# A recommender tower on one core: context's term in one stacked fp32r pass, fewer early lookups, and two more tiles in the plain form

## The chip, the cores and the metric

The kernel runs on one core of one Trainium2 chip. The metric is device time in microseconds, the median of repeated runs. Engines are called as in the profile: PE is TensorE (PEld its weight loads), DVE is VectorE, ACT is ScalarE, POOL is GpSimd, SP is SyncE.

## What is computed

The inputs are 1024 samples. For each, 39 table lookups of 16 numbers give `e` (1024 x 39 x 16). Two layers of products between fields follow, then a sum over the 16 positions, and a small dense network on top:

```python
def _cin_layer(x0, xk, W, b):
    out = jnp.einsum('bhd,bmd,shm->bsd', xk, x0, W) + b[None, :, None]
    return jax.nn.relu(out)
x1 = _cin_layer(x0, x0, W1, b1)          # W1: 128 x 39 x 39
x2 = _cin_layer(x0, x1, W2, b2)          # W2: 128 x 128 x 39
z = jnp.concatenate([x1.sum(axis=-1), x2.sum(axis=-1)], axis=-1)
h = jnp.concatenate([z, dense_ctx], axis=1)          # 256 + 16 features
h = jnp.maximum(h @ W_top1 + b_top1, 0.0)            # 512
h = jnp.maximum(h @ W_top2 + b_top2, 0.0)            # 256
y = h @ W_top3
```

## The kernel before, in words

The samples are cut into 32 tiles of 32; a tile has 512 columns (32 samples x 16 positions) and is worked off in two pairs, so there are 64 pairs. Precision is kept with fp32r matmuls on split operands: a value is split into a high part (an fp32r copy, made by ACT) and a low part (the value less its high part), and a product is the sum of high x high, high x low and low x high. A matmul on plain fp32 operands leaves two records in the profile.

**The way of a tile.** POOL looks up its rows (`look_up`, L418, ten indirect DMAs for each tile, semaphore `s_look`). SP copies them in place with 16 DMAs (L411, `s_put`); for the first two tiles DVE and ACT do it. POOL multiplies out 15 of the products (`multiplied_out`, L361). ACT makes the high part (`high_part`, L604) and two copies of the products' high part (`products_high`, L610); POOL makes the low parts (`low_parts`, L369). All lands in `e_hl`, a ring of 8 buffers. PE transposes it (`turn`, L817). Then come seven steps of layer 1 (`layer1_at`, L859): an expanding matmul (L837), a square on ACT (`square`, L573), and a matmul that adds it up. From tile SOON = 4 on, a square is split: ACT makes the high part and the full square (L584, L585), DVE the low part (L717), and PE runs three fp32r matmuls (L850, L851, L853). Tiles before SOON use one fp32 matmul (L855). ACT and DVE then make the layer's result with its parts (L593, L596, L721).

**The second layer.** A pair has 39 fields, in banks of four: 7 banks "D" that DVE multiplies and adds up (L769, 54 operations a pair, and two at the end, L792 and L796), and 3 banks "A" that ACT scales (L552) and POOL adds up (`middle_fields`, `four_to_two`, `last_two`, `whole_sum`, all L431) to `fsum`. Each bank is 6 fp32r matmuls on PE (L881, L882, L885) into a ring of three: before a bank, PE waits until the bank three places earlier is drained (L876). The order of a pair's ten slots is written out: `DDADDADDAD`. DVE starts a pair from `fsum`; for pairs before LATE = 4 it starts from zero and adds `fsum` at the end (L782).

**What sets the order.** Every engine's program is laid out by pair p and slot s (0 to 9). `layer1_steps` says which layer 1 step stands behind which slot; `high_slots(p)` behind which slots ACT makes the high parts; `split_pair(t)` in which pair tile t is split; `turn_step` where it is transposed; `lookups(p)` how many lookups POOL makes in round p (one at a time between its adds, L503 to L539). POOL's round p holds the adds of pair p + 1. An engine does its instructions in order, so a wait stops all that stands behind it.

**The top layers** run for samples 0 to 511 during pairs 34 to 37, for 512 to 959 during pairs 60 to 63, and for the last 64 at the end. In layer 1 each of four steps has three fp32 matmuls (L914): the two sums, and the context with 16 rows.

Of the kernel before, what the change touches and what calls it, by code (L numbers as in the profile page):

```python
# [11 lines left out]
F32R = mybir.dt.float32r  # L12
# [4 lines left out]
S = 128  # L17
CTX = 16
F1, F2 = 512, 256

# [11 lines left out]
LOOKED = 8  # L32


SOON = 4

# [24 lines left out]

LATE = 4
SLOTS = len(ORDER)
# [120 lines left out]
def lookups(p):  # L184

    return 7 if p < 6 else 6


def high_slots(p):

    return (6, 7) if p == 0 else (0, 1) if SPLIT_IN[p] < SOON else (3, 6)

# [37 lines left out]
def cin_tower(nc, table, ids_first, ids, first_row, w1a, w1b, fold, w2, b2, sel, ident, rows_sum, wt1, wt1c, bt1, wt2, bt2, wt3, ctx_t, out):  # L230
    with ExitStack() as stack:
# [13 lines left out]
        prod = sb("prod", [P, LOOKED, ZP * DT])  # L245
        e_hl = sb("e_hl", [P, LOOKED, P, DT])
        x0t = sb("x0t", [P, 2, N], F32R)
# [31 lines left out]
        wt1_sb = sb("wt1_sb", [P, 2, F1])  # L279
        wt1c_sb = sb("wt1c_sb", [CTX, F1])  # L280
        wt2_sb = sb("wt2_sb", [P, F1 // P, F2])
        wt3_sb = sb("wt3_sb", [P, F2 // P])
        ctx_sb = sb("ctx_sb", [CTX, B])

# [10 lines left out]
        s_const = sem("s_const")  # L295
        s_mlpw = sem("s_mlpw")
        s_rows = sem("s_rows")
        s_look = [sem(f"s_look{t}") for t in range(TILES)]
# [70 lines left out]
        def low_parts(engine, t):  # L369

            done, hl = s_el_first if t < FIRST_TILES else s_el, e_hl[:, t % LOOKED, :, :].rearrange("p m d -> p (m d)")
            engine.wait_ge(s_eh, 3 * t + 1)
            engine.tensor_tensor(hl[:, M * DT:2 * M * DT], e[:, t, :, :].rearrange("p m d -> p (m d)"), hl[:, 0:M * DT],
                                 ALU.subtract).then_inc(done, 1)
            engine.wait_ge(s_eh, 3 * t + 2)
            engine.tensor_tensor(hl[:, ZL * DT:(ZL + ZP) * DT], prod[:, t % LOOKED, :], hl[:, ZH * DT:(ZH + ZP) * DT],
                                 ALU.subtract).then_inc(done, 1)
# [13 lines left out]
        with nc.Block() as block:  # L391
# [25 lines left out]
            def _(pool):  # L417
# [83 lines left out]
                for p in range(PAIRS):  # L501
                    mine, then = SPLIT_IN.get(p), p + 1
                    mine_soon = mine is not None and mine < SOON  # L503
                    ahead = iter(range(n, min(n + lookups(p), TILES * LOOKUPS)))
                    n += lookups(p)

                    def look_ahead(count):
                        for k in itertools.islice(ahead, count):
                            look_up(k)

                    if mine_soon:
                        multiplied_out(nc.gpsimd, mine)
                    look_ahead(1)
                    if mine is not None and not mine_soon:
                        multiplied_out(nc.gpsimd, mine)
                    if then < PAIRS:
                        middle_fields(then)
                    look_ahead(1)
                    if mine_soon:
                        low_parts(nc.gpsimd, mine)  # L520
                    if then < PAIRS:
                        four_to_two(then, 2, 1, 0)
                    look_ahead(1)
                    if then < PAIRS:
                        four_to_two(then, 3, 2, 8)
                    look_ahead(1)
                    if then < PAIRS:
                        last_two(then)
                    look_ahead(1)
                    if then < PAIRS:  # L530
                        whole_sum(then)
                    if p % 2 == 0 and p // 2 + 1 < TILES:
                        position_sum(p // 2 + 1)
                    look_ahead(1)
                    if mine is not None and not mine_soon:
                        low_parts(nc.gpsimd, mine)
                    if p + 2 < PAIRS:
                        first_fields(p + 2)
                    look_ahead(lookups(p))  # L539
# [3 lines left out]
            def _(act):  # L543
# [60 lines left out]
                def high_part(t):  # L604
                    wait_put(act, t)
                    if t >= LOOKED:
                        act.wait_ge(s_full, STAGED["turn", t - LOOKED] + 1)
                    nc.scalar.activation(e_hl[:, t % LOOKED, 0:M, :].bitcast(F32R), e[:, t, :, :], ACT.Copy).then_inc(s_eh, 1)

                def products_high(t):  # L610
# [7 lines left out]
                    for row in (ZH, ZW):  # L618
                        nc.scalar.activation(e_hl[:, t % LOOKED, row:row + ZP, :].bitcast(F32R), src, ACT.Copy).then_inc(s_eh, 1)

# [42 lines left out]
                for p in range(PAIRS):  # L663
                    mine = SPLIT_IN.get(p)
                    for s in range(SLOTS):
# [11 lines left out]
                        for kind, q, j in BANK_SLOTS[1 + SLOTS * p + s]:  # L677
                            if kind == "A":
                                scaled_fields(q, j)
                            elif kind == "L":  # L680
                                last_scaled_fields(j)
                        if mine is not None and s == high_slots(p)[0]:
                            high_part(mine)
# [16 lines left out]
            def _(dve):  # L700
# [11 lines left out]
                def square_low(t, v):  # L712
                    k = C1 * t + v
                    dve.wait_ge(s_sq, splits(t, v))
                    if k >= 2:
                        dve.wait_ge(s_mm1, k - 1)
                    nc.vector.tensor_tensor(zl[:, k % 2, :], ps[:, BK_T, :], zh[:, k % 2, :], ALU.subtract).then_inc(s_zl, 1)  # L717

                def first_layer_low(t):
# [32 lines left out]
                for p in range(PAIRS):  # L752
                    n = p * STT_PER_PAIR
                    last = d_banks(p) - 1
                    for j in range(last + 1):
# [19 lines left out]
                        for at in split_after(p, j):  # L775
                            square_low(*at)
                    for sub in range(2):
                        x2 = ps[:, 2 * (nth % RING) + sub, k * S:(k + 1) * S]
# [21 lines left out]
            def _(pe):  # L800
# [16 lines left out]
                def turn(t):  # L817
# [6 lines left out]
                    for d in range(DT):  # L824
                        mm = nc.tensor.transpose(ps[:, BK_T, d * P:(d + 1) * P],  # L825
                                                 e_hl[:, t % LOOKED, :, d], ident_sb[:])
                    mm.then_inc(s_full, 1)
# [67 lines left out]
                def mlp(g, layer, c):  # L895
                    lo, hi = GROUPS[g]
                    f, y = slice(c * P, (c + 1) * P), ps[:, BK_T, 0:hi - lo]
                    if layer == 1:
                        if c == 0:
                            pe.wait_ge(s_mlpw, 16 * len(mlp_weights))  # L900
                            pe.wait_ge(s_p2t, hi // BT)
                            pe.wait_ge(s_p1, P1_OPS * hi // BT)
                        terms = [(wt1_sb[:, 0, f], p1[:, lo:hi]), (wt1_sb[:, 1, f], p2t[:, lo:hi]),
                                 (wt1c_sb[:, f], ctx_sb[:, lo:hi])]
                    elif layer == 2:
# [43 lines left out]
                pe.wait_ge(s_p1, P1_OPS * TILES)  # L949
                pe.wait_ge(s_mlpw, 16 * len(mlp_weights))  # L950
                for c in range(F1 // P):
                    f = slice(c * P, (c + 1) * P)
# [4 lines left out]
                    nc.tensor.matmul(ps[:, TAIL_1[c], 0:n], wt1_sb[:, 0, f], p1[:, lo:hi], start=True, stop=False)  # L957
                    nc.tensor.matmul(ps[:, TAIL_1[c], 0:n], wt1c_sb[:, f], ctx_sb[:, lo:hi], start=False, stop=False)
                sums(TILES - 1)
# [88 lines left out]
```

## Time and profile before

| | us |
|---|---|
| median of 3 runs | 1210.94 (1210.28 to 1210.98) |
| the profiled execution | 1209.32 |
| its span in the profile | 1207.3 |
| PE busy | 1162.2 |
| DVE busy | 1075.3 |
| POOL busy | 900.6 |
| ACT busy | 692.3 |

The profile shows one execution. Busy times of PE are times in which a matmul is in flight; matmuls are pipelined, so the distance from one start to the next says more than a record's length. A wait is put down to the instruction that came last before it ended.

### The profile page before, as it was taken

How to read it: one execution, taken by the hardware profiler on the slowest of the kernel's cores; microseconds unless marked ns; L12 is line 12 of the kernel's file. 1: busy time of each engine (PE TensorE's matmuls, PEld its weight loads, DVE VectorE, ACT ScalarE, POOL GpSimd, SP SyncE). 2: the span in 40 equal slices, each digit the busy share in tenths (PEclk: the TensorE clock that was granted, in tenths of full speed). 3: DMA queues.
4: the chain of work that ended last, by engine and by line, in shares of the span. 5: the costliest groups of instructions: out<-in, count | busy, mean ns of one | idle time of the engine just before them, and what ended most of it. 6: DMA issues, size and time to landing. Idle time of an engine off the chain costs nothing.

```text
span 1207.3 us, 18938 instructions
## 1 busy us (share of the span) xinstructions
PE 1162.2 (96%) x4952; PEld 898.9 (74%) x4952; DVE 1075.3 (89%) x3811; ACT 692.3 (57%) x2177; POOL 900.6 (75%) x930
## 2 busy tenths in 40 slices
PE   3897999999999999999999999999999999999998
PEld 2575777777777777777777677777778777777766
DVE  4476899999999999999999779999999999999966
ACT  3554565656666556666565555566666566656432
POOL 7898998888888888888887676888876454645432
PEclk9998999999999999999999999999999999999998
DMA  5111111111111111111111100111110000000000
GB/s 180 8 7 7 7 8 6 7 6 7 6 7 8 7 6 7 6 6 7 7 7 6 6 5 5 7 7 7 7 6 2 1 1 1 1 1 1 1 1 1
DMA packets 170249, 11.58 MB, mean 10 GB/s; under 512 B 163630, under 2 KB 169262, under 8 KB 170013
## 3 DMA queue, kind: packets, MB, share of 16 engines
q1 hardware_dynamic: 159901, 7.73, 7.5%
q0 software_dynamic: 10240, 2.64, 2.8%
q8 instruction: 39, 0.64, 0.2%
q14 instruction: 69, 0.57, 0.2%
HBM read 7.92 MB, written 0.00 MB: 7 GB/s over the span
## 4 chain that ended last, share of the span: by engine, by line
PE 59%; DVE 16%; ACT 12%; issue 6%; POOL 6%; DMA 0%; POOLq 0%; DVEq 0%; ACTq 0%; SPq 0%
PE ps L881 16%; PE ps L882 15%; DVE acc L769 15%; PE ps L885 14%; ACT fy L552 9%; POOL looked L422 4%; PE ps L914 3%; PE ps L837 2%; ACT ps L585 2%; ACT zh L584 1%; PE ps L850 1%; PE ps L851 1%; PE ps L853 1%; PE ps L825 1%; POOL fsum L431 1%
## 5 line engine op out<-in xcount | busy, mean ns | idle before, releaser
L769 DVE SCALAR_TENSOR_TENSOR acc<-ps,e,acc 128x128 f32<-128x128 f32 x3186 | 846.9, 342 | 76.6 <-PE ps L885 70.6
L431 POOL TENSOR_TENSOR fy<-fy 128x512 f32<-128x512 f32 (+1 forms) x256 | 403.0, 1574 | 204.7 <-ACT fy L552 196.3
L881 PE MATMUL ps<-w2h,x1h 128*128 128x512 f32 (+1 forms) x1280 | 523.3, 409 | 21.2 <-ACT fy L552 9.9
L882 PE MATMUL ps<-w2l,x1h 128*128 128x512 f32 (+1 forms) x1280 | 496.3, 388 | 0.0
L885 PE MATMUL ps<-w2h,x1l 128*128 128x512 f32 (+1 forms) x1280 | 495.5, 387 | 0.4 <-DVE x1l L721 0.4
L552 ACT ACTIVATE fy<-ps,e 128x128 f32<-128x128 f32 x1536 | 415.8, 387 | 83.0 <-PE ps L885 82.9
L422 POOL DMA_INDIRECT looked<-in_table,rows x320 | 311.6, 974 | 58.3 <-POOL fy L431 23.4
L881 PEld LDWEIGHTS ps<-w2h,x1h 128*128 128x128 f32 x1280 | 241.5, 189 | 125.9 <-DVE acc L769 33.9
L885 PEld LDWEIGHTS ps<-w2h,x1l 128*128 128x128 f32 x1280 | 241.1, 188 | 49.6 <-DVE x1l L721 0.9
L882 PEld LDWEIGHTS ps<-w2l,x1h 128*128 128x128 f32 x1280 | 241.7, 189 | 43.7 <-issue 4.7
L584 ACT ACTIVATE zh<-ps 128x512 fp32r<-128x512 f32 x168 | 103.7, 617 | 247.2 <-PE ps L837 243.2
L717 DVE TENSOR_TENSOR zl<-ps,zh 128x512 fp32r<-128x512 f32 x168 | 114.9, 684 | 9.7 <-ACT ps L585 8.4
L585 ACT ACTIVATE ps<-ps 128x512 f32<-128x512 f32 x168 | 103.7, 617 | 0.0
L837 PE MATMUL ps<-x0t,sel_r 78*128 78x512 f32 x186 | 74.2, 399 | 0.9 <-ACT z L587 0.9
L850 PE MATMUL ps<-zh,w1h 128*128 128x512 f32 x168 | 66.9, 398 | 0.0
L851 PE MATMUL ps<-zh,w1l 128*128 128x512 f32 x168 | 66.4, 395 | 0.0
L853 PE MATMUL ps<-zl,w1h 128*128 128x512 f32 x168 | 66.1, 394 | 0.0
L431 POOL TENSOR_TENSOR fy<-fy,b_sb 128x256 f32<-128x256 f32 x64 | 47.4, 741 | 11.5 <-ACT fy L552 10.8
L431 POOL TENSOR_TENSOR fsum<-fy 128x256 f32<-128x256 f32 x64 | 47.7, 745 | 3.8 <-DVE acc L769 1.7
L593 ACT ACTIVATE x1h<-ps 128x512 fp32r<-128x512 f32 x32 | 19.1, 598 | 43.4 <-PE ps L853 41.7
L769 DVE SCALAR_TENSOR_TENSOR acc<-ps,e,fsum 128x128 f32<-128x128 f32 x120 | 36.2, 343 | 8.5 <-POOL fsum L431 8.5
L837 PEld LDWEIGHTS ps<-x0t,sel_r 78*128 78x128 f32 x186 | 34.9, 188 | 9.1 <-ACT z L587 2.7
(87 smaller groups left out, 624.4 us busy)
## 6 DMA issues: line engine op xcount, KB each, us to landing
e<-looked SPq DMA_DIRECT2D x360, 5.0 KB, 1.9
looked<-in_table,rows POOLq DMA_INDIRECT x320, 2.4
e<-looked SPq DMA_DIRECT2D x120, 4.5 KB, 1.9
w_st<-in_w SPq DMA_DIRECT2D x1, 1728.0 KB, 10.1
wt_sb<-in_wt SPq DMA_DIRECT2D x2, 512.0 KB, 4.1
w_st<-in_w SPq DMA_DIRECT2D x1, 768.0 KB, 5.9
w_sb<-in_w1a SPq DMA_DIRECT2D x1, 448.0 KB, 3.2
w1b_sb<-in_w1b SPq DMA_DIRECT2D x1, 448.0 KB, 3.9
```

The lines of the kernel that those rows point to most:

```text
L422: nc.gpsimd.indirect_dma_start(looked[:, t % LOOKED, j, :], None, table, bass.IndirectOffsetOnAxis(rows[:, t, j:j + 1], 0)).then_inc(s_loo ...
L431: nc.gpsimd.tensor_tensor(out, a, b, ALU.add).then_inc(s_fsum, 1)
L552: nc.scalar.activation(fy[:, p % 2, sub, m - MD, :], ps[:, 2 * (nth % RING) + sub, k * S:(k + 1) * S], ACT.Copy, scale=emb(p, sub, m)).the ...
L584: nc.scalar.activation(zh[:, k % 2, :], src, ACT.Square).then_inc(s_z1, 1)
L585: nc.scalar.activation(src, src, ACT.Square).then_inc(s_sq, 1)
L717: nc.vector.tensor_tensor(zl[:, k % 2, :], ps[:, BK_T, :], zh[:, k % 2, :], ALU.subtract).then_inc(s_zl, 1)
L769: nc.vector.scalar_tensor_tensor(acc[:, sub, :] if m < fields("D", last)[-1] else y, y, emb(p, sub, m), acc[:, sub, :] if m else fsum[:, p ...
L837: nc.tensor.matmul(ps[:, BK_T, :], sel_r[:, v, :], x0t[0:2 * M, t % 2, :], start=True, stop=True).then_inc(s_full, 1)
L850: nc.tensor.matmul(ps[:, BK_ACC1, :], w1h[:, v, :], zh[:, k % 2, :], start=False, stop=False)
L881: nc.tensor.matmul(y, x1h[:, t % 2, at], w2h[:, cols], start=True, stop=False)
L882: nc.tensor.matmul(y, x1h[:, t % 2, at], w2l[:, cols], start=False, stop=False)
L885: mm = nc.tensor.matmul(y, x1l[:, t % 2, at], w2h[:, cols], start=False, stop=True)
```

## The change

Context's term: the host lays the 16 context rows and the 16 weight rows out three times, at rows 0, 32 and 64 of arrays of 80 rows, with zeros between. ACT copies both to fp32r (`context_high`, in pair 14 behind slot 9), DVE puts the low parts of the context into rows 32 to 47 (at the end of pair 16) and those of the weights into rows 64 to 79 (at the end of pair 18). One fp32r matmul of 80 rows then gives the three products.

Early pairs: SOON goes from 4 to 6, so tiles 4 and 5 take the unsplit form; their steps stand every two slots from slot 11 of their tile's stretch on (before: every three from slot 6), their high parts are made in pairs 4 and 6 (before: 3 and 5) behind slots 1 and 4, and they are transposed at slot 0 of the next pair. Tile 3's high parts move from slots 0 and 1 of pair 2 to slots 4 and 5. POOL's low parts of tile 3 move ahead of `middle_fields`. Lookups go from 7 in each of rounds 0 to 5 to 6, 5, 5, 5, 6, 6. LATE goes from 4 to 7. `e_hl` has 4 buffers instead of 8.

```diff
-SOON = 4
+HELD = 4
+SOON = 6
-LATE = 4
+LATE = 7
 def lookups(p):
-    return 7 if p < 6 else 6
+    return 6 if p == 0 or p >= 4 else 5
 def high_slots(p):
-    return (6, 7) if p == 0 else (0, 1) if SPLIT_IN[p] < SOON else (3, 6)
+    return (6, 7) if p == 0 else (4, 5) if p == 2 else (1, 4) if SPLIT_IN[p] < SOON else (3, 6)
+CONTEXT_AT, CONTEXT_LOW = (14, 9), (16, 18)
...
-        e_hl = sb("e_hl", [P, LOOKED, P, DT])
+        e_hl = sb("e_hl", [P, HELD, P, DT])
-        wt1c_sb = sb("wt1c_sb", [CTX, F1])
+        wt1c_sb = sb("wt1c_sb", [CTX_K, F1])
+        wt1c_r = sb("wt1c_r", [CTX_K, F1], F32R)
-        ctx_sb = sb("ctx_sb", [CTX, B])
+        ctx_sb = sb("ctx_sb", [CTX_K, B])
+        ctx_r = sb("ctx_r", [CTX_K, B], F32R)
...
                         multiplied_out(nc.gpsimd, mine)
+                    if p == 2:
+                        low_parts(nc.gpsimd, mine)
                     if then < PAIRS:
                         middle_fields(then)
                     look_ahead(1)
-                    if mine_soon:
+                    if mine_soon and p != 2:
                         low_parts(nc.gpsimd, mine)
...
                 def high_part(t):
                     wait_put(act, t)
-                    if t >= LOOKED:
-                        act.wait_ge(s_full, STAGED["turn", t - LOOKED] + 1)
+                    if t >= HELD:
+                        act.wait_ge(s_full, STAGED["turn", t - HELD] + 1)
...
+                def context_high():
+                    act.wait_ge(s_mlpw, 16 * len(mlp_weights))
+                    nc.scalar.activation(ctx_r[:], ctx_sb[:], ACT.Copy).then_inc(s_ctxh, 1)
+                    nc.scalar.activation(wt1c_r[:], wt1c_sb[:], ACT.Copy).then_inc(s_ctxh, 1)
...
+                        if (p, s) == CONTEXT_AT:
+                            context_high()
...
+                def context_low():
+                    rows = slice(CTX_ROWS[1], CTX_ROWS[1] + CTX)
+                    dve.wait_ge(s_ctxh, 1)
+                    nc.vector.tensor_tensor(ctx_r[rows, :], ctx_sb[rows, :], ctx_r[rows, :], ALU.subtract).then_inc(s_ctxl, 1)
+
+                def context_weights_low():
+                    rows = slice(CTX_ROWS[2], CTX_ROWS[2] + CTX)
+                    dve.wait_ge(s_ctxh, 2)
+                    nc.vector.tensor_tensor(wt1c_r[rows, :], wt1c_sb[rows, :], wt1c_r[rows, :], ALU.subtract).then_inc(s_ctxl, 1)
...
+                    if p == CONTEXT_LOW[0]:
+                        context_low()
+                    elif p == CONTEXT_LOW[1]:
+                        context_weights_low()
                     for sub in range(2):
                         x2 = ps[:, 2 * (nth % RING) + sub, k * S:(k + 1) * S]
...
                             pe.wait_ge(s_mlpw, 16 * len(mlp_weights))
+                            pe.wait_ge(s_ctxl, 2)
...
-                                 (wt1c_sb[:, f], ctx_sb[:, lo:hi])]
+                                 (wt1c_r[:, f], ctx_r[:, lo:hi])]
...
-                    nc.tensor.matmul(ps[:, TAIL_1[c], 0:n], wt1c_sb[:, f], ctx_sb[:, lo:hi], start=False, stop=False)
+                    nc.tensor.matmul(ps[:, TAIL_1[c], 0:n], wt1c_r[:, f], ctx_r[:, lo:hi], start=False, stop=False)
...
+    for row in CTX_ROWS:
+        wt1c[row:row + CTX], ctx_t[row:row + CTX] = x["W_top1"][2 * S:], x["dense_ctx"].T
```

## Rows read from the trace of the kernel before

**Rows 1.** The page: busy time by engine, share of the span, instructions.
```profile
PE 1162.2 (96%) x4952; PEld 898.9 (74%) x4952; DVE 1075.3 (89%) x3811; ACT 692.3 (57%) x2177; POOL 900.6 (75%) x930
```
**Rows 2.** Stretches: from:to, length, busy by engine (instructions), PE clock, DMA share, GB/s.
```profile
300.00:334.90 34.90, 34.55 (x153) 27.30 (x152) 33.53 (x121) 21.24 (x67) 29.98 (x32) 1.00 0.14 7
```
**Rows 3.** Waits: waiter, what it waited for, us in total, times, longest.
```profile
DVE acc L769 <- PE ps L885: 70.6, 57, 9.0
```
**Rows 4.** Timeline of PE, 92 to 102 us: start, length, instruction [idle before].
```profile
92.74 0.39 PE L885 MATMUL ps<-w2h,x1l 128*128 128x512 f32 x1
100.57 0.79 PE L881 MATMUL ps<-w2h,x1h 128*128 128x512 f32 x1 [7.44 <-ACT fy L552]
```
**Rows 5.** Stretches, columns as in rows 2.
```profile
100.60:104.60 4.00, 4.00 (x11) 3.26 (x12) 0.00 (x0) 0.80 (x4) 3.83 (x4) 0.51 0.18 6
```
**Rows 6.** Timeline of ACT, 84 to 101 us.
```profile
90.84 0.34 ACT L608 ACTIVATE e_hl<-e 128x156 fp32r<-128x156 f32 x1 [4.29 <-DMA e<-looked]
...
98.06 0.40 ACT L619 ACTIVATE e_hl<-prod 128x60 fp32r<-128x60 f32 x2 [5.92 <-POOL prod L367]
98.36 2.15 ACT L552 ACTIVATE fy<-ps,e 128x128 f32<-128x128 f32 x8
```
**Rows 7.** Timeline of SP's DMA issues, 70 to 95 us.
```profile
77.52 11.38 SPq L411 DMA_DIRECT2D e<-looked  x16
```
**Rows 8.** Timeline of POOL, 79 to 99 us.
```profile
96.73 0.96 POOL L422 DMA_INDIRECT looked<-in_table,rows  x1 [0.16 <-POOL fy L431]
97.71 0.32 POOL L367 TENSOR_TENSOR prod<-e 128x60 f32<-128x60 f32 x1
```
**Rows 9.** Timeline of DVE, 84 to 113 us.
```profile
105.67 5.26 DVE L769 SCALAR_TENSOR_TENSOR acc<-ps,e,acc 128x128 f32<-128x128 f32 x20 [9.04 <-PE ps L885]
...
112.43 0.60 DVE L766 TENSOR_SCALAR acc<-ps,e 128x128 f32<-128x128 f32 x2
```
**Rows 10.** Timeline of PE, 74 to 78 us.
```profile
75.94 0.40 PE L837 MATMUL ps<-x0t,sel_r 78*128 78x512 f32 x1
76.18 1.02 PE L855 MATMUL ps<-z,w_sb 128*128 128x512 f32 x2
...
77.27 0.40 PE L882 MATMUL ps<-w2l,x1h 128*128 128x512 f32 x1
```
**Rows 11.** Stretches, columns as in rows 2.
```profile
112.40:219.00 106.60, 105.59 (x458) 82.84 (x456) 99.12 (x357) 63.28 (x200) 94.92 (x100) 1.00 0.14 7
```
**Rows 12.** Timeline of POOL, 154 to 172 us.
```profile
154.26 0.33 POOL L367 TENSOR_TENSOR prod<-e 128x60 f32<-128x60 f32 x1
...
171.18 2.41 POOL L431 TENSOR_TENSOR fy<-fy 128x1024 f32<-128x1024 f32 x1
```
**Rows 13.** Timeline of POOL, 146.5 to 151 us.
```profile
147.99 0.74 POOL L480 TENSOR_TENSOR xs<-x 128x256 f32<-128x256 f32 x1
...
150.14 0.96 POOL L422 DMA_INDIRECT looked<-in_table,rows  x1
```
**Rows 14.** Timeline of PE, 653 to 657 us.
```profile
653.54 1.02 PE L914 MATMUL ps<-p,wt_sb 128*128 128x512 f32 x2
...
655.35 1.12 PE L914 MATMUL ps<-ctx_sb,wt1c_sb 16*128 16x512 f32 x2
656.40 0.50 PE L881 MATMUL ps<-w2h,x1h 128*128 128x512 f32 x1
656.74 0.40 PE L882 MATMUL ps<-w2l,x1h 128*128 128x512 f32 x1
```
**Rows 15.** Timeline of DVE, 1128 to 1190 us.
```profile
1176.05 2.16 DVE L769 SCALAR_TENSOR_TENSOR acc<-ps,e,acc 128x128 f32<-128x128 f32 x8 [2.24 <-PE ps L885]
```
**Rows 16.** Groups of instructions by shape: count, busy us, mean ns, idle before.
```profile
L730 DVE TENSOR_TENSOR w_sb<-w_sb,w1b_sb 128x896 f32<-128x896 f32 x1 | 1.1, 1092 | 2.7 <-DMA fold_sb<-in_fold 2.7
```
**Rows 17.** Timelines of DVE and POOL, 19.5 to 31 us.
```profile
23.72 3.76 DVE L709 SCALAR_TENSOR_TENSOR w2l<-w_st,w2h 128x3456 fp32r<-128x3456 f32 x1
...
24.11 4.19 POOL L422 DMA_INDIRECT looked<-in_table,rows  x1 [0.30 <-issue]
```

More of the change, by code:

```diff
@@ L18 @@
 CTX = 16
+CTX_ROWS = (0, 32, 64)
+CTX_K = CTX_ROWS[-1] + CTX
 F1, F2 = 512, 256
@@ L296, in cin_tower @@
         s_mlpw = sem("s_mlpw")
+        s_ctxh = sem("s_ctxh")
+        s_ctxl = sem("s_ctxl")
         s_rows = sem("s_rows")
@@ L369, in low_parts @@
         def low_parts(engine, t):
-            done, hl = s_el_first if t < FIRST_TILES else s_el, e_hl[:, t % LOOKED, :, :].rearrange("p m d -> p (m d)")
+            done, hl = s_el_first if t < FIRST_TILES else s_el, e_hl[:, t % HELD, :, :].rearrange("p m d -> p (m d)")
             engine.wait_ge(s_eh, 3 * t + 1)
@@ L605, in high_part @@
                     wait_put(act, t)
-                    if t >= LOOKED:
-                        act.wait_ge(s_full, STAGED["turn", t - LOOKED] + 1)
-                    nc.scalar.activation(e_hl[:, t % LOOKED, 0:M, :].bitcast(F32R), e[:, t, :, :], ACT.Copy).then_inc(s_eh, 1)
+                    if t >= HELD:
+                        act.wait_ge(s_full, STAGED["turn", t - HELD] + 1)
+                    nc.scalar.activation(e_hl[:, t % HELD, 0:M, :].bitcast(F32R), e[:, t, :, :], ACT.Copy).then_inc(s_eh, 1)
                 def products_high(t):
@@ L618, in products_high @@
                     for row in (ZH, ZW):
-                        nc.scalar.activation(e_hl[:, t % LOOKED, row:row + ZP, :].bitcast(F32R), src, ACT.Copy).then_inc(s_eh, 1)
+                        nc.scalar.activation(e_hl[:, t % HELD, row:row + ZP, :].bitcast(F32R), src, ACT.Copy).then_inc(s_eh, 1)
+                def context_high():
+                    act.wait_ge(s_mlpw, 16 * len(mlp_weights))
+                    nc.scalar.activation(ctx_r[:], ctx_sb[:], ACT.Copy).then_inc(s_ctxh, 1)
+                    nc.scalar.activation(wt1c_r[:], wt1c_sb[:], ACT.Copy).then_inc(s_ctxh, 1)
                 def sums_turned(t):
@@ L825, in turn @@
                         mm = nc.tensor.transpose(ps[:, BK_T, d * P:(d + 1) * P],
-                                                 e_hl[:, t % LOOKED, :, d], ident_sb[:])
+                                                 e_hl[:, t % HELD, :, d], ident_sb[:])
                     mm.then_inc(s_full, 1)
@@ L950, in _ @@
                 pe.wait_ge(s_mlpw, 16 * len(mlp_weights))
+                pe.wait_ge(s_ctxl, 2)
                 for c in range(F1 // P):
@@ L1025 @@
     first_row = np.repeat(first_row.reshape(LOOKUPS, Q).T, BT, axis=0)
+    wt1c, ctx_t = np.zeros((CTX_K, F1), np.float32), np.zeros((CTX_K, B), np.float32)
+    for row in CTX_ROWS:
+        wt1c[row:row + CTX], ctx_t[row:row + CTX] = x["W_top1"][2 * S:], x["dense_ctx"].T
     arrays = {
@@ L1031 @@
         "sel": selection(), "ident": np.eye(P, dtype=np.float32), "rows_sum": np.tile(np.eye(BT, dtype=np.float32), (Q, 1)),
-        "wt1": x["W_top1"][:2 * S].reshape(2, S, F1).transpose(1, 0, 2), "wt1c": x["W_top1"][2 * S:],
+        "wt1": x["W_top1"][:2 * S].reshape(2, S, F1).transpose(1, 0, 2), "wt1c": wt1c,
         "bt1": x["b_top1"].reshape(F1 // P, P).T,
@@ L1036 @@
         "wt3": x["W_top3"].reshape(F2 // P, P).T,
-        "ctx_t": x["dense_ctx"].T,
+        "ctx_t": ctx_t,
     }
```

## The prediction

> **What bounds the kernel now.** I read the page first: the matmul engine is busy for 96% of the span, VectorE for 89%, GpSimd for 75% [rows 1]. A busy matmul engine proves little by itself, so next came the table of stretches. One tile (two pairs) takes 34.9 us in the middle of the run, with 34.55 us busy on PE and 33.53 us on DVE [rows 2]: both are nearly full, PE sets the pace, and DVE follows so closely that a microsecond more on it in one place will mostly show. The table of waits then says where time is lost in one piece: DVE waited 9.0 us once for PE [rows 3]. The timeline of PE shows the hole behind it, 7.44 us of waiting for ACT's scaling, from 92.97 to 100.57 us [rows 4], in pair 2 before its slot 5 (L881 needs the bank that ACT drains at L552). Behind it the clock is at 0.51, the lower level of 1.2 GHz, for 4 us; its 11 matmul records run at half speed, which costs some 2 us [rows 5].
>
> Why was ACT late? Its timeline in pair 2 has two waits ahead of the scaling: 4.29 us for tile 3's placed rows (L608), then 5.92 us for tile 3's products from POOL (L619) [rows 6]. SyncE issues the 16 copies of tile 3 in 11.4 us and is done at 88.9 [rows 7]; POOL comes to the products only at 97.71, because adds and lookups stand before them without a gap [rows 8]. So the early hole is ACT's order (the high part at slots 0 and 1) and POOL's load.
>
> **The change, part by part.** All against the profiled execution (1209.3 us), which is 1.6 us under the median of 1210.9.
>
> (a) High part of tile 3 at slots 4 and 5, and its low parts moved up on POOL. ACT first does first_layer(2) and the scaling for slot 2, so the wait for the copies stops nothing that PE needs before slot 7. POOL loses one lookup in pair 0 and two in pair 1; one is 0.98 us from start to start, 0.16 us more where a start gap goes with it [rows 8], so 3.4 us for three, and the products come at 94.3 instead of 97.71. ACT is at slot 5 until about 96.8 (the bank is ready at 94.6, eight scalings are 2.2 us [rows 6]), so the product copy no longer waits; POOL's low_parts(3) waits for it until about 97.2, some 1.4 us, with middle_fields(3) behind it in POOL's queue, which even so starts at 97.5 and not at 100.6. What is late next is DVE: it stood 9.04 us before 105.67, and needs 6.76 us from there to the start of pair 3 at 112.43 [rows 9]. Without the hole PE would deliver pair 2's last bank at about 100.1, so DVE runs on from 96.6 and starts pair 3 at 103.4. Gain 9.0 us; the clock's 2 us lie inside it, since DVE becomes the bound for a moment.
>
> (b) SOON from 4 to 6: tiles 4 and 5 take the plain fp32 form. On PE a step's one fp32 matmul (two records) takes 0.86 us: from 76.18 to 77.27 less the 0.23 of the matmul that follows [rows 10]. It takes the place of three fp32r ones at 0.23, 0.69 in all; 12 steps x 0.17 = 2.0 us more. In return DVE loses 12 subtractions, which stood at 0.6 us each, and ACT 12 squares. The stretch of pairs 3 to 8 holds 105.59 us of PE work in 106.6 [rows 11], but with restarts after DVE's waits of about 0.1 each inside the busy time; I take 1.3 us of waits to go. Net cost 0.7 us; bounds 2.0 (no wait goes) and -0.3.
>
> (c) LATE from 4 to 7 adds two small DVE operations in pairs 4 to 6 (some 0.25 us of spacing each, 1.5 us) and takes away their wait for fsum at the start. DVE has 7 us more room there by (b): nothing, up to 0.5 if DVE is full after all.
>
> (d) Lookups. POOL took 16.9 us for the round from one product (154.26) to the next middle_fields (171.18), with seven lookups and one low_parts [rows 12]: 6.9 for the lookups and 1.1 for products and low parts leave 8.9 for the adds; even rounds have 2.15 for position_sum as well [rows 13]. Laid end to end behind low_parts(3) at 97.5 (four lookups left, adds, position_sum: 112.4; then five and adds: 126.2; six and all: 144.2; six and adds: 159.0) POOL comes to the products of tile 4 at 126.2 and of tile 5 at 159.0. PE starts pair 3 at 100.9, and needs 13.5 us for a pair's banks (60 matmuls at 0.23, six of them shorter), with a turn and five steps of 1.09 some 18.6, with the last two steps 15.9: pair 4 at 119.5, pair 6 at 153.9. ACT wants the products four slots later, at 127.2 and 161.3. fsum(7) comes 13.5 us into round 6, at 172.5, where DVE wants it at about 172. All fit, none by much. Tile 3's last lookup keeps its place, so its copies land as before. Tile 6's last lookup comes in pair 6 and its copies end at about 176.5, where ACT wants them at 175.5: inside the ring's three slots. Lookups end one pair later: 0.2 us.
>
> (e) HELD 4 halves the memset at the start, which lies ahead of a DMA wait: nothing. The bigger context arrays add 0.38 MB to SyncE's burst at 19 us; the next lookups that anybody waits for end at 32 us: nothing, at most 0.5.
>
> (f) Context term in one pass. Before, context's matmul takes 655.35 to 656.40, and the L881 behind it 0.34 us instead of 0.23; ahead of it stands 0.09 (the first two take 1.72 of the 1.81 us from 653.54) [rows 14]. So one step spends 1.05 + 0.11 + 0.09 = 1.25 us on it, where an fp32r pass costs 0.23. Saving 1.02 for each of four steps, and by columns (448 of 512) 0.89 for each of the next four: 7.6 us. These bubbles of 0.2 to 0.3 stand only around this 16-row load; the 128-row fp32 steps at L855 have none [rows 10]. If they stayed, the saving would be the columns alone, 0.86 - 0.23 = 0.63 and 0.55: 4.7 us, the lower bound. I take the upper one, 7.6, since the 78-row fp32r matmul at L837, nearest to the new pass in form and rows, also runs free of them: the next one starts 0.24 us behind it [rows 10]. PE is the bound in both stretches: even in the last pairs DVE waits 2.24 us for it at 1176 [rows 15], so what PE saves reaches the end. The tail's context matmuls lie before a wait for DVE: nothing.
>
> (g) Splitting context. ACT makes two copies (1.0 and 0.6 us) in pair 14, between squares three slots apart: hidden. DVE has 1024 and 512 columns at the ends of pairs 16 and 18. The nearest row is an add of 896 columns, 1.09 us [rows 16], which gives 1.2 and 0.65: 1.85 less the overlap, 1.7 us. It stands before the drain of the pair's last bank, and DVE had 1.4 us of room in a whole tile; bounds 0.3 and 1.9, I take 1.7.
>
> Here a rule speaks against the change. A POOL lookup that met DVE's long low-part operation (23.72, 3.76 us, two inputs from SBUF) took 4.19 us [rows 17] instead of 0.96 [rows 8]. A delay like that at pairs 16 and 18 would be at most the two operations' own length, 1.9 us on POOL, and counts only if fsum becomes late by it. The Trainium skill, SBUF — State Buffer, section on who interferes with whom, says that a VectorE instruction with two SBUF inputs and a GpSimd instruction that reads SBUF shut each other out for the whole instruction. By that rule, the sum would be up to 1.9 us worse; the trace agrees that such waits happen.
>
> Sum: -9.0 + 0.7 + 0.2 - 7.6 + 1.7 = -14.0, so 1195.3 for a profiled execution and 1196.9 for the median; I say 1197.0.
>
> **Rivals.**
> 1. The hole moves instead of going. Ahead of slot 44 and slot 64 ACT needs POOL's products, with margins of only 1 to 3 us in (d), and turn(3) needs low_parts(3). Against it: the ring covers three slots, some 4 us. Half of (a) lost: -9.5, 1201.5.
> 2. The lockout of [rows 17] comes fully on the path: 1.9 us more, 1198.9. Against it: at odd pairs DVE rarely waits for fsum.
> 3. Slower than before: POOL falls behind for good in pairs 2 to 6, since it now stands waiting for ACT in pair 2. The point is a product copy (slot 44) that waits more than 4.2 us, three slots of 1.4; I reckon below 0.5. Then (a)'s 9.0 stays lost and one more hole of 9.0 opens: +9.0 + 0.7 + 0.2 - 7.6 + 1.7 = +4.0, 1214.9.
> 4. The change doesn't do what it says: the stacked pass costs as much as the fp32 one. Then only (a) to (e) and (g) count: -6.4, 1204.5. Against it: the fp32r matmul at L837 has 78 rows and takes 0.24 us [rows 10].
>
> **How the numbers follow.** A measurement of this kernel tells 0.2% (2.4 us) from no change. Forecast 0.64, rival 1 0.15, rival 2 0.10, rival 3 0.04, rival 4 0.04; 0.03 for a total near zero. The range starts from the sum of the better bounds (-9.0 - 0.3 + 0.2 - 7.6 + 0.3 = -16.4, 1194.5, with 2 us for DVE waits that I had as full cost) at 1192.5, and reaches to 1204.0, which takes in rivals 1 and 2 and the worse bounds together (-9.0 + 2.0 + 0.5 + 0.2 + 0.5 - 4.7 + 1.9 = -8.6, 1202.3). Faster 0.93, same 0.03, slower 0.04.
>
> **What would show it.** In the new profile: PE without a hole above 1 us in 92 to 102 us and the clock at 1.00 there; pair 3 starts on DVE near 103.4; the product copy of tile 3 without a wait, POOL waiting 1.4 us before low_parts(3); L855 with 72 records instead of 48; the tile period at 34.9 us as before; four steps of L914 near 675 and four near 1145 each 0.9 to 1.0 us shorter, context as single records; a DVE operation of 1.2 us near 348 us with a PE wait of about 1 us behind it. The forecast is wrong if a PE wait above 2 us stands anywhere between 100 and 200 us, if the tile period of the middle differs from 34.9 us, or if bubbles stay around the context matmul.

## The result, and the profile after

The changed kernel takes 1196.01 us in the median (four runs, 1195.4 to 1197.02) where the kernel before takes 1210.96 (1210.28 to 1211.69): ratio 0.9877, 95% interval 0.986 to 0.9894. The profiled execution took 1195.4, its span 1193.6, so 13.7 us less span. The forecast was 1197.0, its range 1192.5 to 1204.0.

The page and the waits that stood first [rows 1, 3], of the changed kernel (waits: waiter, what it waited for, us in total, times, longest):

```profile
PE 1152.4 (97%) x4928; PEld 894.1 (75%) x4928; DVE 1071.0 (90%) x3807; ACT 689.9 (58%) x2167; POOL 904.2 (76%) x930
```
```profile
DVE acc L801 <- PE ps L921: 63.5, 64, 5.2
```

PE has 9.8 us less busy time for 13.7 us less span, and the longest wait of DVE for PE fell from 9.0 to 5.2. Where the hole stood [rows 4, 5, 2], the table of stretches (from:to, length, busy by engine, PE clock, DMA share, GB/s) and PE's timeline now show:

```profile
92.00:102.00 10.00, 9.33 (x43) 7.36 (x42) 9.98 (x38) 5.02 (x21) 9.32 (x12) 1.00 0.03 3
300.00:334.90 34.90, 34.57 (x152) 27.26 (x151) 33.48 (x120) 22.73 (x69) 29.95 (x32) 1.00 0.11 6
```
```profile
100.28 0.50 PE L917 MATMUL ps<-w2h,x1h 128*128 128x512 f32 x1 [0.67 <-DVE acc L801]
```

The clock is 1.00 where it was 0.51, PE's longest wait in these 10 us is 0.67 and is for DVE, PE waits nowhere over 1 us between 85 and 200 us, and the middle of the run is what it was. ACT and POOL in pair 2 [rows 6, 8]:

```profile
89.89 2.18 ACT L567 ACTIVATE fy<-ps,e 128x128 f32<-128x128 f32 x8 [0.30 <-issue]
91.91 0.38 ACT L623 ACTIVATE e_hl<-e 128x156 fp32r<-128x156 f32 x1
...
96.23 0.45 ACT L634 ACTIVATE e_hl<-prod 128x60 fp32r<-128x60 f32 x2
```
```profile
94.58 0.33 POOL L380 TENSOR_TENSOR prod<-e 128x60 f32<-128x60 f32 x1
...
96.07 0.54 POOL L386 TENSOR_TENSOR e_hl<-e,e_hl 128x156 f32<-128x156 f32 x1
...
96.89 2.40 POOL L444 TENSOR_TENSOR fy<-fy 128x1024 f32<-128x1024 f32 x1
```

ACT scales first and copies afterwards; neither the copy of the rows nor that of the products waits (4.29 and 5.92 us before).

To see where the 13.7 us come from I took the start of every pair on DVE in both traces. The gain (before less after), summed up to that pair:

| pair | 0 | 2 | 3 | 5 | 9 | 16 | 17 | 19 | 34 | 38 | 60 | 62 | span |
|---|---|---|---|---|---|---|---|---|---|---|---|---|---|
| us | -0.36 | 0.54 | 9.67 | 10.95 | 8.62 | 8.50 | 7.11 | 6.21 | 5.93 | 9.89 | 9.45 | 13.08 | 13.7 |

Each step of the prediction has its place in it: the hole (pair 2 to 3), the two plain tiles (to 9), the subtractions (16 to 17 and 18 to 19), the two groups of the top layer (34 to 38, 60 to 62). The 0.54 us before pair 2 and the 0.63 behind pair 62 belong to no step; the steps and what lies between them come to 12.5 us.

### The profile page after: what moved, and what is told of

Same layout as the page of the kernel before. It is cut to its first block, busy times and chain, and to the rows that moved or that the text cites. A ratio compares the mean times of both kernels' runs of the same rounds, so it can differ in the third digit from the quotient of the medians.

```text
span 1193.6 us, 18875 instructions
## 1 busy us (share of the span) xinstructions
PE 1152.4 (97%) x4928; PEld 894.1 (75%) x4928; DVE 1071.0 (90%) x3807; ACT 689.9 (58%) x2167; POOL 904.2 (76%) x930
## 4 chain that ended last, share of the span: by engine, by line
PE 64%; DVE 13%; ACT 12%; issue 6%; POOL 4%; DMA 0%; POOLq 0%; ACTq 0%; SPq 0%; DVEq 0%
PE ps L917 18%; PE ps L918 16%; PE ps L921 16%; DVE acc L801 12%; ACT fy L567 9%; POOL looked L435 3%; PE ps L951 3%; PE ps L873 3%; PE ps L891 2%; ACT ps L600 1%; PE ps L886 1%; PE ps L887 1%; PE ps L889 1%; ACT zh L599 1%; PE ps L861 1%
## 5 line engine op out<-in xcount | busy, mean ns | idle before, releaser
L918 PE MATMUL ps<-w2l,x1h 128*128 128x512 f32 (+1 forms) x1280 | 495.1, 387 | 0.0
L918 PEld LDWEIGHTS ps<-w2l,x1h 128*128 128x128 f32 x1280 | 240.7, 188 | 46.6 <-issue 7.6
L599 ACT ACTIVATE zh<-ps 128x512 fp32r<-128x512 f32 x156 | 96.4, 618 | 228.9 <-PE ps L873 228.9
L739 DVE TENSOR_TENSOR zl<-ps,zh 128x512 fp32r<-128x512 f32 x156 | 106.6, 683 | 8.4 <-ACT ps L600 6.5
L600 ACT ACTIVATE ps<-ps 128x512 f32<-128x512 f32 x156 | 96.2, 617 | 0.0
L886 PE MATMUL ps<-zh,w1h 128*128 128x512 f32 x156 | 61.9, 397 | 0.0
L887 PE MATMUL ps<-zh,w1l 128*128 128x512 f32 x156 | 61.7, 395 | 0.0
L889 PE MATMUL ps<-zl,w1h 128*128 128x512 f32 x156 | 61.4, 393 | 0.0
L602 ACT ACTIVATE z<-ps 128x512 f32<-128x512 f32 x36 | 21.9, 610 | 40.5 <-PE ps L873 34.7
```

Of the source, the lines that this page charges most:

```text
L599: nc.scalar.activation(zh[:, k % 2, :], src, ACT.Square).then_inc(s_z1, 1)
L600: nc.scalar.activation(src, src, ACT.Square).then_inc(s_sq, 1)
L886: nc.tensor.matmul(ps[:, BK_ACC1, :], w1h[:, v, :], zh[:, k % 2, :], start=False, stop=False)
L918: nc.tensor.matmul(y, x1h[:, t % 2, at], w2l[:, cols], start=False, stop=False)
```

## The experiments

Three sets ran, each with the kernel before on the same chip. In the first two it took 1210.3 and 1210.7 us. In the third it took 1214.7, and the profiled kernels of that set all lose 6.1 to 7.4 us on the changed kernel's trace between pairs 0 and 1, ahead of all that is studied; why stays open. Its four kernels are therefore compared with each other, and one of them stands for the changed kernel. The changed kernel itself ran in none of the three sets: where x5, x6 and x8 are set against its median, two sets are compared in which the kernel before differs by 0.2 us. "The gain at pair n" is as in the table above.

**The two halves alone.** x1 is the changed kernel with the early pairs as before (SOON 4, LATE 4, lookups, `high_slots` and the place of the low parts undone); x2 is the kernel before with just these five.

> The kernel before with the context part of the change alone (stacked pass, its copies and subtractions, four buffers of e_hl; SOON, LATE, lookups, slots and low parts as before). My theory: the two parts are independent, since the early hole closes long before the context is touched. The pass gives 7.6 us, the tail 0.6, the two subtractions on DVE cost 2.3 (1.39 and 0.88 as seen in the changed kernel): 5.9 us less than before, near 1203.4 in a profiled execution, with the 7.4 us hole still at 93 us. Rival: part of the 13.7 us came from an interplay, and this alone gives under 4 us.

> The kernel before with the early part alone (SOON 6, LATE 7, fewer lookups, tile 3's slots and low parts; context as before). My theory: pair 3 starts on DVE 9.0 to 9.7 us earlier, 1.0 is lost again by pair 9, 0.4 by the later end of the lookups: 8.2 us less than before, near 1201.1. Rival: the shorter fill of e_hl and the context's place matter in the early stretch, then it gives under 7 us.

x1: 1204.42, ratio 0.9952 (0.9935 to 0.9969), 5.9 us less than before. From pair 16 to 19 it loses 2.26, from 34 to 38 it gains 3.88, from 60 to 62 3.63. x2: 1202.04, ratio 0.9929 (0.9913 to 0.9946), 8.2 us less; 8.54 at pair 3, 7.53 at pair 9. The two add up to 14.1 of the 14.95 in medians. In spans they give only 5.0 and 6.6 of the 13.7, but 1.6 of the missing 2.2 lie before pair 2 and behind pair 62, which no step touches. Step by step they agree with the whole: 9.14 against 9.13 from pair 2 to 3, 2.26 lost against 2.29 from 16 to 19, 3.88 less 0.12 against 3.96 from 34 to 38, 3.63 less 0.19 against 3.63 from 60 to 62. No interplay larger than these differences is to be seen.

**One piece of the early half at a time.** x3, the kernel before with

```diff
-    return (6, 7) if p == 0 else (0, 1) if SPLIT_IN[p] < SOON else (3, 6)
+    return (6, 7) if p == 0 else (4, 5) if p == 2 else (0, 1) if SPLIT_IN[p] < SOON else (3, 6)
```

> The kernel before with one edit: tile 3's high parts behind slots 4 and 5 of pair 2 instead of 0 and 1. Theory A (ACT's order makes the hole): the 7.4 us hole is gone; what is late next is POOL's low_parts(3), which still stands behind an add and a lookup, so the transposition at slot 30 waits some 2 us; pair 3 starts 7 us earlier, total 6 to 7 us less. Theory B (POOL's load makes the hole): POOL still reaches the products at 97.7, and the hole shrinks by under 3 us.

1210.3, ratio 1.0 (0.9989 to 1.001); the profiled execution was its quickest, 1208.1. Theory A has the hole right and the total wrong; theory B has the hole wrong. The hole of pair 2 goes as in the whole change, 9.22 us at pair 3, and 7.8 of them are lost again at once: 1.42 at pair 4. DVE's and PE's timelines of x3:

```profile
129.65 0.61 DVE L769 SCALAR_TENSOR_TENSOR acc<-ps,e,fsum 128x128 f32<-128x128 f32 x2 [6.77 <-POOL fsum L431]
```
```profile
131.86 0.79 PE L881 MATMUL ps<-w2h,x1h 128*128 128x512 f32 x1 [5.42 <-DVE acc L769]
```

POOL was always late: the kernel before gets this sum at 131.06, x3 at 129.65, hardly sooner. Before, the hole gave it the time, and DVE waited 0.47 us for the sum. With the hole gone and LATE at 4, DVE stands at the start of pair 4 for POOL's sum, and PE behind DVE.

x4, the kernel before with only fewer lookups:

```diff
-    return 7 if p < 6 else 6
+    return 6 if p == 0 or p >= 4 else 5
```

> The kernel before with one edit: the lookups of the changed kernel (6, 5, 5, 5, 6, 6 instead of 7 in rounds 0 to 5). Theory A: ACT still waits for tile 3's copies until 90.8 and then for the products, which now come at 94.6 instead of 97.7; the hole shrinks by 3.1 to about 4.3 us, total 3 to 4 us less. Theory B: the hole nearly goes, total 7 us or more less.

1217.01, ratio 1.0055 (1.0035 to 1.0075), 6.7 us slower; both theories had it faster. The hole shrinks from 7.44 to 4.75 us, near theory A's 4.3, and then ACT stands for the rows of tiles 4 and 5, whose high parts are still due in pairs 3 and 5; the gain falls from 3.58 at pair 3 to -7.18 at pair 6. ACT's timeline of x4:

```profile
120.69 0.33 ACT L608 ACTIVATE e_hl<-e 128x156 fp32r<-128x156 f32 x1 [6.25 <-DMA e<-looked]
...
161.47 0.34 ACT L608 ACTIVATE e_hl<-e 128x156 fp32r<-128x156 f32 x1 [4.91 <-DMA e<-looked]
```

**One piece taken back.** x5 is the changed kernel with `SOON = 4`, x6 with `LATE = 4`, x8 with the lookups of before (7 in rounds 0 to 5).

> The changed kernel with SOON back at 4: tiles 4 and 5 in the split form. PE saves 12 x 0.17 = 2.0 us of matmuls. Theory A (my term b: SOON 6 costs PE 2.0 and gives back waits for DVE): with DVE and ACT full again in pairs 3 to 8, waits for DVE come back, and the total is within 1 us of the changed kernel. Rival: the plain form is a pure cost once the hole is gone, and the total falls by 2 us. Second rival: without DVE's room the two more late adds make DVE the bound, and the total rises by over 1.5 us.

> The changed kernel with LATE back at 4: pairs 4 to 6 start from fsum. Theory A: POOL gives fsum(4) at 123.9, fsum(5) near 139 and fsum(6) near 155.6, where DVE starts at 120.8, 137.9 and 156.0: DVE waits 3 us at pair 4, 1 to 2 at pair 5, and since DVE has room in odd pairs about 2 us of it stay; total 1 to 3 us more. Rival: LATE is worth nothing (under 0.5 us), as I had it.

> The changed kernel with the lookups of before (7 in each of rounds 0 to 5). Tests the margin of rival 1 and 3: POOL is up to 3.4 us later in pair 2 and falls back 2 us more in each of rounds 2 and 3. Theory A (three slots of room, 4.2 us, then PE stops): the products of tile 3 come at 98 where ACT wants them at 96.2, low parts at 99.6: below 1 us at pair 3; by pair 4 POOL is 7 to 8 us late, products of tile 4 come near 132 where ACT wants them at 125: PE stops for 3 us or more there, total 2 to 5 us more. Rival: POOL's idle time takes it up, and the total stays within 1 us.

x5: 1207.34, ratio 0.9972 (0.9958 to 0.9985), 11.3 us more than the changed kernel's median. The second rival had the direction, no theory the cause or the size. ACT's and PE's timelines of x5:

```profile
120.18 0.33 ACT L623 ACTIVATE e_hl<-e 128x156 fp32r<-128x156 f32 x1 [10.56 <-DMA e<-looked]
```
```profile
121.05 0.80 PE L873 MATMUL ps<-x0t,sel_r 78*128 78x512 f32 x1 [5.13 <-ACT z L602]
...
162.16 0.50 PE L917 MATMUL ps<-w2h,x1h 128*128 128x512 f32 x1 [2.39 <-ACT fy L567]
```

Tile 4's rows are in place at 120.2, since its last lookup now comes a round later. With SOON 4 ACT asks for them at 109.6, in pair 3; with SOON 6 at 122.78, in pair 4, and waits for nothing. Tile 5's rows are late too, by 4.68 us at 158.71, with PE's second wait behind them. That, more than its arithmetic, is what SOON 6 is for (x9 below takes the two apart).

x6: 1198.37, ratio 0.9897 (0.9868 to 0.9926), 2.4 us more than the changed kernel by medians (two executions, and the intervals of the ratios overlap), 2.0 by spans and 1.9 by the starts of pairs 3 to 9: at the start of pair 4 DVE waits for the sum that LATE 7 lets it add at the end.

```profile
124.11 0.61 DVE L801 SCALAR_TENSOR_TENSOR acc<-ps,e,fsum 128x128 f32<-128x128 f32 x2 [3.01 <-POOL fsum L444]
```

x8: 1204.14, ratio 0.9942 (0.9919 to 0.9964), 8.1 more by medians and 7.0 by spans, where theory A had the cause but only 2 to 5 us. It loses nothing before pair 4, 5.5 in pair 4 (the gain is 10.08 at pair 4 and 5.32 at pair 5, where the changed kernel has 10.22 and 10.95), and 7.2 by pair 7. So the hole of pair 2 needs no fewer lookups to close (9.14 us from pair 2 to 3); they matter from pair 4 on. ACT's and PE's timelines of x8:

```profile
133.33 0.40 ACT L634 ACTIVATE e_hl<-prod 128x60 fp32r<-128x60 f32 x2 [5.36 <-POOL prod L380]
```
```profile
136.03 0.76 PE L917 MATMUL ps<-w2h,x1h 128*128 128x512 f32 x1 [3.42 <-ACT fy L567]
```

This is the mechanism of rival 3: a wait of ACT of 5.36 us opened a hole of 3.42 on PE, where ACT's waits of 2.56 us for tile 4's rows and 2.36 for its products in x3 opened none. Two other runs lie between: ACT's 4.68 us for tile 5's rows in x5 opened 2.39 on PE, and its 4.91 in x4 opened 2.61.

```profile
164.92 0.50 PE L881 MATMUL ps<-w2h,x1h 128*128 128x512 f32 x1 [2.61 <-ACT fy L552]
```

Each hole is 1.9 to 2.3 us shorter than the wait behind it. The point therefore lies between 2.56 and 4.68 us, and by these differences nearer the lower end than rival 3's 4.2, three slots of 1.4.

**The context pass.** x7 is the kernel before, fp32 matmuls and all, with the context arrays padded with zeros from 16 to 80 rows (no split, no fp32r):

```diff
-        wt1c_sb = sb("wt1c_sb", [CTX, F1])
-        ctx_sb = sb("ctx_sb", [CTX, B])
+        wt1c_sb = sb("wt1c_sb", [80, F1])
+        ctx_sb = sb("ctx_sb", [80, B])
```

> The kernel before with context still one plain fp32 matmul, but over 80 rows, of which 64 are zeros. It separates the two reasons for the 1.01 us that a step saved. Theory A: the bubbles around the context matmul (0.09 ahead, 0.21 behind) come with the 16-row weight load, and go with 80 rows: a step takes 2.81 us instead of 3.20 from the first matmul to the second one behind it, total 2 to 2.5 us less than before. Theory B: they come with the order (fp32 to fp32r, or the wait behind the step): a step stays at 3.2 us, total within 0.5 us of before.

1207.47, ratio 0.9973 (0.9959 to 0.9986): 3.3 us less by medians, 2.8 by spans, though it only multiplies more zeros. PE's timeline, first of x7, then of the changed kernel (before: [rows 14]):

```profile
653.87 1.02 PE L914 MATMUL ps<-p,wt_sb 128*128 128x512 f32 x2
...
655.59 1.02 PE L914 MATMUL ps<-ctx_sb,wt1c_sb 80*128 80x512 f32 x2
656.05 0.79 PE L881 MATMUL ps<-w2h,x1h 128*128 128x512 f32 x1
656.68 0.39 PE L882 MATMUL ps<-w2l,x1h 128*128 128x512 f32 x1
```
```profile
647.59 1.02 PE L951 MATMUL ps<-p,wt_sb 128*128 128x512 f32 x2
...
648.91 0.80 PE L951 MATMUL ps<-ctx_r,wt1c_r 80*128 80x512 f32 x1
...
649.78 0.40 PE L918 MATMUL ps<-w2l,x1h 128*128 128x512 f32 x1
```

From the step's first matmul to the L882 (L918) behind it: 3.20 us before, 2.81 padded, 2.19 in one fp32r pass. The other three steps of the first group give 0.30 to 0.38 and 0.64 to 0.65 for the two differences. So 0.3 to 0.4 us a step are bubbles that belong to the 16-row matmul and go with 80 rows in fp32 as well; 0.62 to 0.65 is the pass itself. No number of rows between 16 and 80 was tried.

**The move of the low parts, and the price of the plain form** (third set). x12 is the changed kernel with tile 3's low parts back behind `middle_fields`; x9 has tiles 4 and 5 split again, at the slots of SOON 6:

```diff
 def is_split(t, v):
-    return t >= SOON and v in SPLIT
+    return t >= 4 and v in SPLIT
```

> The changed kernel with POOL's low parts of tile 3 back behind middle_fields and a lookup. Theory A: POOL then ends them at 100.5, and the transposition at slot 30 starts at about 101.7: nothing waits, total within 0.5 us of the changed kernel; the move had worth only as insurance. Rival: they end later than slot 30 and PE waits, total 1 us or more up.

> The changed kernel, with the squares of tiles 4 and 5 split again but everything at the changed kernel's slots (steps every two slots, high parts in pairs 4 and 6). It separates SOON's arithmetic from its schedule. Theory A (what SOON 6 bought is the later due slot of the copies, seen when SOON 4 cost 12 us; the plain form costs PE 2.0): PE has 2.0 us less, DVE 7.2 us and ACT 6 us more in pairs 5 to 8, DVE becomes the bound there, total within 1.5 us of the changed kernel either way. Rival: the plain form itself is what the early pairs need, and the total rises by over 4 us.

x12: 1201.65, ratio 0.9892 (0.9872 to 0.9911). Against the changed kernel's trace its shift is flat through the place of the move, 6.75 us at pair 1 and 6.70 at pair 9: the move is worth nothing here. POOL made the low parts at 103.78, and the transposition at 108.51 did not wait for them. x12 therefore stands for the changed kernel in this set.

x9: 1203.96, ratio 0.9911 (0.9891 to 0.993), 2.3 us more than x12 by medians (two executions each, and the intervals overlap) and 1.6 by spans. Its shift grows by 1.6 over pairs 5 to 9. The stretch of pairs 5 to 8, first of x9 and then of the changed kernel:

```profile
144.50:218.60 74.10, 71.01 (x313) 56.59 (x311) 69.49 (x246) 45.50 (x139) 61.74 (x66) 1.00 0.15 7
```
```profile
137.90:210.40 72.50, 71.28 (x301) 54.84 (x299) 62.63 (x234) 39.53 (x127) 61.74 (x66) 1.00 0.15 7
```

PE is busy 0.3 us less in x9, not 2.0 as worked out for the fp32r form, and stands idle 3.1 us of the stretch instead of 1.2. DVE is busy 6.9 us more; 1.6 us is what it comes to.

**A better place for the subtractions.** In the changed kernel DVE waits 1.67 us for PE in each of pairs 3, 5 and 7 (its operation at 113.33, 148.43 and 184.55), where tiles 3, 4 and 5, in the plain form, ask no low part of it. x10 puts the two subtractions there:

```diff
-CONTEXT_AT, CONTEXT_LOW = (14, 9), (16, 18)
+CONTEXT_AT, CONTEXT_LOW = (4, 6), (5, 7)
...
+                        if (p, j) == (CONTEXT_LOW[0], 3):
+                            context_low()
+                        elif (p, j) == (CONTEXT_LOW[1], 3):
+                            context_weights_low()
```

x11 has `LATE = 8` in addition, so that DVE adds pair 7's sum at the end.

> The changed kernel with context's copies in pair 4 behind slot 6, and its two subtractions on DVE in pairs 5 and 7 behind the fourth bank, where DVE waits 1.67 us for PE each time. Theory: the 1.39 and 0.88 us that they cost at pairs 16 and 18 go, since they fall into waits: 2.0 to 2.3 us less than the changed kernel, near 1193.3 in a profiled execution. Rival: the pair of subtractions costs the same wherever it stands, because DVE sets the pace of the stretch: no change.

> As the run before, and LATE 8: pair 7 no longer starts from fsum, for which DVE waits 1.28 us in the changed kernel. Theory: two small operations of 0.53 us replace the wait: 0.5 to 0.8 us less than the run before. Rival: the wait moves to pair 8, which starts from fsum too: no change.

x10: 1200.41, ratio 0.9882 (0.9865 to 0.9898), 1.2 us less than x12 by medians and 1.4 by spans, where 2.0 to 2.3 were expected. DVE's timeline of x10:

```profile
153.95 1.22 DVE L744 TENSOR_TENSOR ctx_r<-ctx_sb,ctx_r 16x1024 fp32r<-16x1024 f32 x1
155.59 4.23 DVE L801 SCALAR_TENSOR_TENSOR acc<-ps,e,acc 128x128 f32<-128x128 f32 x16 [0.42 <-PE ps L921]
```

The 1.67 us of waiting became 1.22 of work and 0.42 of waiting. By the starts of the pairs x10 loses 0.04 between pairs 3 and 9, and gains 2.16 on the changed kernel between 16 and 19: the size expected. The rest went ahead of pair 1, where x10 already stood 0.33 us behind x12, and in the tail.

x11: 1199.69, ratio 0.9875 (0.9859 to 0.9892), 0.7 less than x10 and 2.0 less than x12. DVE's wait at pair 7 is gone; 0.47 us of it return at pair 8, which now is the first that starts from POOL's sum. The shift against the changed kernel shrinks by 0.96 between pairs 3 and 9. It is the fastest of its set. It ran beside x12, which does the changed kernel's work in another place, and not beside the changed kernel; against the kernel before, its ratio is the changed kernel's (0.9875 and 0.9877), so that it beats the changed kernel rests on x12 standing for it.

## Why the prediction was right

The sum was -14.0 and the span gave -13.7. That they meet within 0.3 is in part luck: 1.2 of the 13.7 lie before pair 2 and behind pair 62, where no step is at work, and the stretch between gave 12.5, which is 1.5 less than the sum. By its steps:

(a) **-9.0, right.** 9.13 from pair 2 to pair 3; pair 3 starts at 102.76 where 103.4 was said, since 0.54 had been gained before. The products came at 94.58 (said: 94.3). Wrong inside it: POOL did not wait 1.4 us for ACT before the low parts. The first of them (96.07) needs only ACT's copy of the rows, made at 91.91, and the copy of the products stood at 96.23 and not at 96.8, so `middle_fields` started at 96.89 instead of 97.5. x12 shows that this order was worth nothing either way. And of the three parts of the step the slots alone did it: x3, with nothing but them, and x8, with all lookups back, give the same 9.1 us from pair 2 to 3.

(b) **+0.7, right in size, wrong in meaning.** From pair 3 to 9 the change loses 1.05, and in the same pairs stands DVE's wait of 1.28 of (d). But the step priced SOON as arithmetic alone. x9 is the test of that part: at the same slots the plain form does not cost 0.7 but saves 1.6 us, better than the better bound of -0.3 (whose 2.3 us of waits stand in no row). The matmuls' price is there, 0.15 of the 0.17 us a step (a plain step takes 1.32 us from its expanding matmul to the second one behind it, 145.76 to 147.08 in the changed kernel, a split one 1.17, 153.14 to 154.31 in x9), but DVE's 6.9 us of room are worth more. And x5 shows that SOON 6 as a whole carries 11.3 us by medians, 12.1 by spans; 1.6 of it is the form (x9), the rest its slots and its later due time. The prediction worked out when tile 3's copies land and never asked it of tile 4 under the fewer lookups of (d); x4 and x5 are that question asked twice.

(c) **0, right in the sum, wrong by 1.9 to 2.4 us as the worth of LATE.** LATE was costed by its extra operations, and the value of the wait that it takes away was left out, though (a) brings DVE to pair 4 sooner than POOL's pace allows: by 6.77 us in x3, by 3.01 in x6. It made no difference to the sum because the whole change was summed with the hole gone once, not part by part.

(d) **+0.2, nearly right.** POOL came to the products of tiles 4 and 5 at 124.53 and 157.53 (said: 126.2 and 159.0), and neither ACT copy waited. For fsum(7) DVE waited, 1.28 us where half a microsecond was reckoned:

```profile
174.33 0.61 DVE L801 SCALAR_TENSOR_TENSOR acc<-ps,e,fsum 128x128 f32<-128x128 f32 x2 [1.28 <-POOL fsum L444]
```

The laying end to end took POOL for never waiting; it stood 2.89 us for ACT's scaling before 161.88. x8 shows what the fewer lookups carry in the changed kernel, 7 to 8 us. The laying out of PE's pair 3 does not add up either: 13.5 and five steps of 1.09 are 18.9 before the transposition, not 18.6. The later end of the lookups came to 0.3 for 0.2 said: the last one stands in pair 48 instead of 46, and there the gain falls by 0.5 and comes back by 0.2 until pair 50, as it does in x2, x4 and every other run with fewer lookups and in none with those of before. Another 0.3 between pairs 32 and 33 is not theirs, since x8 has it and x2 and x4 don't; its cause stays open.

(e) **0**: nothing of it is to be seen; the start of pair 0 is 0.36 us later, and at pair 1 the change is 0.60 ahead. These 0.9 us also come in x1, x4, x6 and x8 and not in x2, x3, x5 and x7, which fits none of the edits; the cause stays open.

(f) **-7.6, right.** 3.96 from pair 34 to 38 and 3.63 from 60 to 62, 7.6 in all; the first four steps are 0.95 to 1.02 us shorter and the next four 0.93 to 0.94, for 1.02 and 0.89 said. That the bubbles of 0.2 to 0.3 come from the 16-row load was a guess from where they stood; x7 shows it, 0.3 to 0.4 a step. ACT's two copies (1.08 and 0.65 us near 314) are hidden, as said.

(g) **+1.7, mis-sized: 2.27 measured** (1.39 from pair 16 to 17 and 0.88 from 18 to 19), above the bound of 1.9. The durations were right:

```profile
349.65 1.22 DVE L744 TENSOR_TENSOR ctx_r<-ctx_sb,ctx_r 16x1024 fp32r<-16x1024 f32 x1
350.90 0.29 DVE L832 TENSOR_SCALAR p<-ps 128x128 f32<-128x128 f32 x1
```

The step took off an overlap. In fact the operation stands alone: DVE's next one starts 1.25 us after it, whereas its neighbours otherwise overlap each other (the one at 351.22 takes 0.29 and the next starts 0.21 behind it). I read it so that an inserted operation costs its length and the overlap that it breaks; no run takes the two apart. The "1.4 us of room in a whole tile" did not help: PE, three banks ahead at most, stood still behind it, about as long as was said there.

```profile
351.56 0.50 PE L917 MATMUL ps<-w2h,x1h 128*128 128x512 f32 x1 [1.18 <-DVE p L828]
```

**The rivals.** Rivals 1 and 3 name real mechanisms of this kernel that the change steps over: x6, x8 and x5 are each one removed safeguard away, and cost 2, 8 and 11 us. Rival 4 is excluded by the step of 2.19 us. Rival 2, the lockout, happened off the path. The POOL add of 128 x 128 beside DVE's subtraction took 1.46 us, the one beside the second subtraction 0.93, and the 30 others 0.46:

```profile
349.73 1.46 POOL L493 TENSOR_TENSOR xt<-xs 128x128 f32<-128x128 f32 x1
```

It delayed no sum that anybody waited for: DVE waits 0.41 us for POOL at the start of pair 18, as at pairs 20 and 22 (0.40 and 0.38) and as before the change (0.40). The rule of the Trainium skill (SBUF — State Buffer, who interferes with whom) says just this of an instruction pair like these, and the trace agrees; for the path it was worth nothing.

The last 0.6 us (13.08 at pair 62, 13.7 in the span) lie in the tail, where the granted clock falls from 1.00 to 0.50 at other moments: 7.2 us before the end in the changed kernel's trace, 10.6 in that of the kernel before. The other traces bear it out. In x5, x8 and x12 it falls 7.6 to 8.1 us before the end, and their tails are 0.2 to 0.4 us shorter than before; in the other nine it falls 9.1 to 10.6 us before it, and their tails are as before within 0.06. It goes with the execution and not with an edit: x1 and x2, the two halves, have nothing of it.

## What to carry to other kernels

A full, in-order pipeline has deadlines: for each piece that is moved or thinned out, write down when the data lands and when each later consumer asks, for all tiles and not only the one with the hole. When a hole is closed, everything that used to hide in it (here POOL's lag of 7 us) has to be moved out of the way in the same change; tried one by one, such parts measure zero or worse (x3: 0.0, x4: +6.7 us) and together with the other pieces of the early half give 8.2 (x2). And an operation put on a nearly full engine costs its full length unless it is placed where that engine is seen to wait.

## What the runs showed of the hardware

- An fp32 matmul with 16 rows costs 0.3 to 0.4 us more around it than the same with 80 rows, 64 of them zeros (3.20 against 2.81 us for the first step). Padding alone gained 3.3 us in 1210.7.
- VectorE's instructions back to back overlap: 16 multiply-adds take 4.23 us here, 0.26 each, though one alone stands at 0.34 in the groups and at 0.6 for two. A 16-row operation in such a stream cost 1.39 us for a length of 1.22, and 0.88 for 0.68.
- A lookup's issue on POOL beside DVE's two-input subtraction kept its 0.95 us in x10 (at 153.76), while the add behind it took 1.58 instead of 1.30. The 4.19 us of [rows 17] are therefore not shown to come from the two inputs as such.
- The granted clock falls near the end of every trace, 7.2 to 10.6 us before the last instruction. Where it falls 8.1 us before it or later, the tail is 0.2 to 0.6 us shorter than where it falls earlier.
